# Pass 1's down projection in three parts, y evicted by halves, and a new order of the queues

## The chip, the cores and the metric

The kernel runs on one core of one Trainium2 chip. The metric is device time in microseconds, the median of three runs.

## The reference, cut to what matters

x has 4 batches of 1024 tokens with 128 features, in fp32. The block is feed-forward, mixer, feed-forward, each with a residual:

```python
x = x + 0.5 * ffn(layernorm(x))
x = x + mixer(layernorm(x))
x = x + 0.5 * ffn(layernorm(x))

def ffn(h):                      # for each batch
    logits = h.mean(axis=1) @ gate_w          # 8 experts
    top_w, top_i = top_k(softmax(logits), 2)  # one pair of experts for a batch
    for e in top_i:
        hmid = gelu(h @ w1[e] + b1[e])        # 128 -> 512
        out += weight_of(e) * (hmid @ w2[e] + b2[e])   # 512 -> 128
```

The mixer normalises, runs a causal convolution of 4 taps, silu, a projection to dt, v and gate, a rotation of v, a decaying scan over time, a mix of the heads, and an output projection.

## The kernel before

There are 8 passes: pass q is the first feed-forward of batch q for q below 4, and the second one of batch q - 4 otherwise. A pass has 8 slots, for 2 experts with 4 blocks of 128 hidden features each. Slot s = 8q + t is, on TensorE, `up(s)`: 6 matmuls of 512 columns into `hid_ps` (w1 and z are each split into a high and a low part in a shorter format, and three of the products are summed). ScalarE's `gelu(s)` evicts it into `hid`. TensorE's `down(s)` adds w2's block into `y_ps`. `down` has two forms:

- by token (`TOKEN_PASSES`, passes 0 to 4): hid is the weights operand, tile by tile, in fp32: 8 matmuls, 16 instructions. y has tokens on its partitions, as x has. GpSimd's `token_bias` adds the bias by a broadcast DMA, and VectorE's `update_x` adds y.
- feature by token: y has features on its partitions. In a slot whose place in its expert is under `PARTS[q]`, ScalarE makes `hid_hi` (`s_hi`), VectorE `hid_lo` (`s_lo`), and `down` runs three terms (high by high, low weight by high, high weight by low) in two halves. w2 is split the same way, by ScalarE (`f_split_w2`) and VectorE (`f_scale_w2`). At the end of the pass ScalarE's `pass_out` (`y_out`) evicts y into `yt` with its bias (`f_bias`), `post` (`y_turn_y`) turns it back by 8 transposes into `aux_ps`, and `update_x` (`y_update`) adds it.

The mixer of batch b runs in between, from `m_stats` to `m_add`; its matmuls and the transposes of z (`f_norm`), the routing (`f_route`) and `post` share `aux_ps`, which is handed on when its last reader is done. In the first passes all 8 experts' w1 are also split ahead (`c_pre_hi`, `c_pre_lo`, `c_pre_out`) for the later passes. `c_split_rest` splits the first pass's experts.

The order on each engine is written out by hand. Each engine walks over ticks; a slot is 40 ticks. `up(s)` and `gelu(s)` stand at tick 40 s + 40, `down(s)` at 40 s + 98, or 40 s + 132 in three parts. Everything else stands at the tick that `AT[engine][step][index]` gives. A tick isn't a time: it only orders the instructions of one engine, and semaphores do the waiting. Engines run their queues in order, so an instruction that waits holds back all behind it.

The last three slots (`TAIL`) run by token into four quarters of two tiles each, added and stored by `update_tail` and `store_quarter`.

## Time and profile before

| | us |
|---|---|
| median of 3 runs | 259.94 (259.83 to 260.12) |
| the profiled execution | 259.85 |
| its span, first to last instruction | 258.1 |
| TensorE busy | 250.5 |
| VectorE busy | 211.5 |
| ScalarE busy | 195.1 |
| GpSimd busy | 83.0 |

The profile is of one execution. An engine's busy time counts its instructions, not its waits. The granted clock of TensorE is 0.998 of full speed over the span, so 2.4 GHz nearly throughout.

### The profile page before, as it was taken

What the parts mean: (1) busy time and instruction counts of PE and PEld (TensorE: products, weight loads), DVE (VectorE), ACT (ScalarE), POOL (GpSimd) and SP (SyncE); (2) the same over time, 40 slices, a digit from 0 to 9 for tenths busy, and PEclk for the clock granted to TensorE, in tenths of its full rate; (3) what the DMA queues carried; (4) which work ended last, traced back from release to release, by engine and by line L of the source; (5) the groups of instructions that cost most, each with busy time, mean ns of one, the idle gap of its engine ahead of it and who ended that gap; (6) DMA issues with size and microseconds to landing.
All of it is one profiled execution on the core that took longest, in us unless ns stands there. A gap on an engine that the chain in (4) does not pass through costs nothing.

```text
span 258.1 us, 4609 instructions
## 1 busy us (share of the span) xinstructions
PE 250.5 (97%) x1540; PEld 217.1 (84%) x1540; DVE 211.5 (82%) x536; ACT 195.1 (76%) x236; POOL 83.0 (32%) x90
## 2 busy tenths in 40 slices
PE   7899999999999999999999999999999999999994
PEld 6879999998998979899979899888678687887893
DVE  4767587798589799999999999999999997675612
ACT  1354665866999877969848989999989957979550
...
GB/s 188 190 280 317 114 128 333 186 192 242 27 0 1 22 113 214 57 28 22 247 0 0 85 0 0 247 0 0 0 11 238 0 0 3 169 228 10 3 81 83
DMA packets 21975, 26.18 MB, mean 101 GB/s; under 512 B 1280, under 2 KB 17152, under 8 KB 21952
## 3 DMA queue, kind: packets, MB, share of 16 engines
...
q10 hardware_dynamic: 1232, 0.55, 0.8%
q8 instruction: 12, 0.20, 0.3%
...
## 4 chain that ended last, share of the span: by engine, by line
PE 90%; ACT 3%; DMA 2%; issue 2%; DVE 1%; SPq 0%; ACTq 0%
PE hid_ps L839 32%; PE y_ps L867 28%; PE y_ps L892 10%; PE aux_ps L978 5%; PE aux_ps L934 4%; PE aux_ps L1010 3%; PE aux_ps L999 3%; DMA xt<-x_dram 1%; PE hid_ps L911 1%; PE y_ps L911 1%; PE aux_ps L959 1%; ACT hid L633 1%; ACT late L723 1%; DMA m_tok<-wpack_dram 1%; PE y_ps L1022 1%
## 5 line engine op out<-in xcount | busy, mean ns | idle before, releaser
L839 PE MATMUL hid_ps<-z_hi,w_parts 128*128 128x512 f32 x256 | 83.9, 410 | 0.4 <-ACT w_parts L586 0.4
L867 PEld LDWEIGHTS y_ps<-w_sb,hid 128*128 128x128 f32 x640 | 77.1, 192 | 4.3 <-DMA w_sb<-wpack_dram 0.7
L867 PE MATMUL y_ps<-w_sb,hid 128*128 128x128 f32 x640 | 78.1, 275 | 0.3 <-ACT hid L633 0.3
L633 ACT ACTIVATE hid<-hid_ps,w_sb 128x1024 f32<-128x1024 f32 x56 | 61.8, 1109 | 16.7 <-PE hid_ps L839 16.4
L839 PEld LDWEIGHTS hid_ps<-z_hi,w_parts 128*128 128x128 f32 x256 | 45.2, 189 | 9.5 <-issue 1.4
L839 PE MATMUL hid_ps<-z_lo,w_parts 128*128 128x512 f32 x128 | 40.1, 394 | 0.0
L1217 DVE TENSOR_TENSOR hid_lo<-hid,hid_hi 128x1024 fp32r<-128x1024 f32 x19 | 22.9, 1220 | 7.8 <-ACT hid_hi L640 7.8
L839 PEld LDWEIGHTS hid_ps<-z_lo,w_parts 128*128 128x128 f32 x128 | 24.0, 188 | 5.6
L640 ACT ACTIVATE hid_hi<-hid 128x1024 fp32r<-128x1024 f32 x19 | 19.6, 1055 | 1.3 <-PE y_ps L892 1.2
L480 POOL TENSOR_SCALAR bias_tok<-w_sb,coef 128x128 f32<-128x128 f32 x10 | 7.2, 730 | 38.7 <-DMA w_sb<-wpack_dram 24.8
L1104 DVE TENSOR_SCALAR f_tok<-xt,f_mv,f_rstd 128x128 f32<-128x128 f32 x64 | 17.6, 353 | 2.0 <-POOL f_rstd L458 1.9
L1083 DVE BATCH_NORM_STATS2 f_stat<-xt 128x6 f32<-128x128 f32 x64 | 13.3, 283 | 5.7 <-DMA xt<-x_dram 5.6
L524 POOL TENSOR_SCALAR small<-mix_tmp 128x32 f32<-128x32 f32 x4 | 4.3, 1083 | 40.7 <-DVE cumd L1331 40.7
L1288 DVE SCALAR_TENSOR_TENSOR xc<-xs,vec_sb,xc 128x1024 f32<-128x1024 f32 x12 | 15.3, 1277 | 1.8 <-ACT xc L686 1.7
L468 POOL TENSOR_SCALAR f_ve<-f_mv 128x8 f32<-128x8 f32 x7 | 2.4, 343 | 43.3 <-DVE f_mv L1086 43.2
L458 POOL TENSOR_TENSOR f_rstd<-f_ve,neg_half 128x8 f32<-128x8 f32 (+1 forms) x9 | 14.6, 1624 | 3.3 <-DVE f_ve L1090 2.8
L633 ACT ACTIVATE hid<-hid_ps,b_first 128x1024 f32<-128x1024 f32 x8 | 8.9, 1110 | 6.4 <-PE hid_ps L839 6.3
L678 ACT ACTIVATE xt<-xt,m_shift,m_gain 128x128 f32<-128x128 f32 x32 | 12.7, 483 | 0.0
L892 PE MATMUL y_ps<-hid_hi,w_hi 128*128 128x512 f32 x38 | 12.5, 409 | 0.0
L892 PE MATMUL y_ps<-hid_lo,w_hi 128*128 128x512 f32 x38 | 11.9, 394 | 0.0
L892 PE MATMUL y_ps<-hid_hi,w_lo 128*128 128x512 f32 x38 | 11.9, 393 | 0.0
L1119 DVE TENSOR_TENSOR z_lo<-f_tok,z_hi 128x1024 fp32r<-128x1024 f32 x7 | 8.6, 1233 | 3.2 <-ACT z_hi L568 3.0
...
## 6 DMA issues: line engine op xcount, KB each, us to landing
...
w_sb<-wpack_dram SPq DMA_DIRECT2D x6, 258.5 KB, 4.2
...
```

What stands on the lines that cost most here:

```text
L458: nc.gpsimd.tensor_tensor(f_rstd[:, tiles], f_ve[:, tiles], neg_half[:, 0, tiles], ALU.pow).then_inc(done, 1)
L633: nc.scalar.activation(hid[:, slot % HBUF, :], hid_ps[:, slot % 2, :], ACT.Gelu, bias=bias).then_inc(hid_ready, 1)
L640: nc.scalar.activation(hid_hi[:, slot % 2, :], hid[:, slot % HBUF, :], ACT.Copy).then_inc(hid_hi_ready, 1)
L678: nc.scalar.activation(xt[:, b, t, :], xt[:, b, t, :], ACT.Identity, bias=m_shift[:, t:t + 1], scale=m_gain[:, t:t + 1]).then_inc(x_plus_h, 1)
L839: last = nc.tensor.matmul(hid_ps[:, slot % 2, cols], w, z[:, q % 2, cols], start=first, stop=end)
L867: last = nc.tensor.matmul(y_ps[:, cols], hid[:, slot % HBUF, cols], w_sb[:, q % 2, k, W2_AT + f * P:W2_AT + (f + 1) * P], start=t == 0 and ...
L892: last = nc.tensor.matmul(y_ps[:, cols], wt, src[:, cols], start=t == 0 and i == 0, stop=slot + 1 in (SLOTS * (q + 1), TAIL[0]) and end)
L978: last = nc.tensor.matmul(aux_ps[:, cols], wt[:, w, :], z[:, cols], start=first, stop=end)
L1083: V.bn_stats(f_stat[:, t, :], xt[:, b, t, :]).then_inc(f_stats_step, 1)
L1104: V.tensor_scalar(f_tok[:, t, :], xt[:, q % B, t, :], f_mv[:, t, 0:1], f_rstd[:, t:t + 1], ALU.subtract, ALU.mult).then_inc(f_norm_done, 1)
L1217: V.tensor_tensor(hid_lo[:, slot % 2, :], hid[:, slot % HBUF, :], hid_hi[:, slot % 2, :].bitcast(F32), ALU.subtract).then_inc(hid_lo_ready, 1)
L1288: V.scalar_tensor_tensor(xc[:, :], xs[:, k:k + N], conv_w[:, k:k + 1], xc[:, :], ALU.mult, ALU.add).then_inc(conv_step, 1)
```

## The change

Pass 1 leaves the passes by token, and all its slots run in three parts (`PARTS[1]` = 4). It gets `f_split_w2`, `s_hi`, `s_lo`, `f_bias` on VectorE, `y_out` and `y_turn_y`, and loses GpSimd's `token_bias`. In each pass with y feature by token, the last slot that `post` covers runs all terms of its first half before those of the second, `y_half_up` tells ScalarE that the first half is up, `pass_out` evicts y in two halves, and the next pass's `down` and `post` wait for each half by itself. The four loads of the first batch are dealt out in another way over the queues of SP and ScalarE. The last additions and stores cover 3, 2, 2 and 1 tiles instead of 2 each. Nearly all positions in `AT` are new; of them the diff shows those of the steps spoken of here.

```diff
@@ -42,90 +42,92 @@
-TOKEN_PASSES = (0, 1, 2, 3, 4)
-
-PARTS = {0: 0, 1: 0, 2: 0, 3: 0, 4: 0, 5: 3, 6: 4, 7: 4}
+TOKEN_PASSES = (0, 2, 3, 4)
+
+PARTS = {0: 0, 1: 4, 2: 0, 3: 0, 4: 0, 5: 3, 6: 4, 7: 4}
 AT = {
     "pe": {
-        "f_norm": {1: 189, 2: 389, 3: 809, 4: 1149, 5: 1509, 6: 1829, 7: 2166},
-        "m_dt": {0: 649, 1: 1029, 2: 1349, 3: 1726},
-        "m_v": {0: 689, 1: 1069, 2: 1409, 3: 1766},
-        "y_turn_y": {5: 2206, 6: 2426, 7: 2600},
+        "f_norm": {1: 169, 2: 329, 3: 849, 4: 1209, 5: 1449, 6: 1829, 7: 2166},
+        "f_route": {1: 189, 2: 369, 3: 929, 4: 1229, 5: 1529, 6: 1860, 7: 2186},
+        "m_norm": {0: 566, 1: 909, 2: 1169, 3: 1489},
+        "m_dt": {0: 749, 1: 1029, 2: 1349, 3: 1726},
+        "m_v": {0: 769, 1: 1069, 2: 1369, 3: 1766},
+        "m_gate": {0: 889, 1: 1289, 2: 1589, 3: 1926},
+        "m_out": {0: 1009, 1: 1329, 2: 1700, 3: 2048},
+        "y_turn_y": {1: 735, 5: 2086, 6: 2406, 7: 2600},
...
     "dve": {
-        "c_split_rest": {0: 90, 1: 115},
-        "c_pre_lo": {0: 309, 1: 317, 2: 366, 3: 377, 4: 490, 5: 496, 6: 502, 7: 556},
-        "f_bias": {5: 1837, 6: 2190, 7: 2383},
-        "m_stats": {0: 400, 1: 751, 2: 1057, 3: 1366},
-        "m_normalise": {0: 453, 1: 842, 2: 1146, 3: 1446},
-        "m_silu": {0: 611, 1: 998, 2: 1329, 3: 1658},
-        "m_silu_lo": {0: 640, 1: 1018, 2: 1345, 3: 1698},
-        "y_update": {0: 384, 1: 722, 2: 1028, 3: 1352, 4: 1668, 5: 2315, 6: 2515, 7: 2584},
...
+        "c_proj": {0: 112},
+        "c_split_rest": {0: 118, 1: 123},
+        "c_mixer": {0: 133},
+        "c_pre_lo": {0: 265, 1: 273, 2: 281, 3: 391, 4: 433, 5: 462, 6: 526, 7: 556},
+        "f_stats": {1: 85, 2: 219, 3: 342, 4: 1095, 5: 1355, 6: 1748, 7: 2090},
+        "f_scale_w2": {0: 147, 1: 364, 2: 754, 3: 1032, 4: 1382, 5: 1736, 6: 2046, 7: 2324},
+        "f_normalise": {1: 152, 2: 288, 3: 727, 4: 1198, 5: 1405, 6: 1823, 7: 2150},
+        "f_route": {1: 202, 2: 535, 3: 943, 4: 1262, 5: 1555, 6: 1884, 7: 2202},
+        "f_split_z": {1: 206, 2: 540, 3: 955, 4: 1307, 5: 1541, 6: 1923, 7: 2260},
+        "f_coef": {1: 259, 2: 690, 3: 978, 4: 1352, 5: 1667, 6: 1990, 7: 2315},
+        "f_bias": {1: 608, 5: 1966, 6: 2145, 7: 2462},
+        "m_stats": {0: 470, 1: 756, 2: 1044, 3: 1385},
+        "m_normalise": {0: 563, 1: 842, 2: 1152, 3: 1475},
+        "m_clip": {0: 613, 1: 947, 2: 1229, 3: 1520},
+        "m_conv1": {0: 656, 1: 968, 2: 1266, 3: 1559},
+        "m_conv2": {0: 675, 1: 982, 2: 1299, 3: 1580},
+        "m_conv3": {0: 710, 1: 992, 2: 1314, 3: 1615},
+        "m_silu": {0: 737, 1: 1009, 2: 1329, 3: 1658},
+        "m_silu_lo": {0: 749, 1: 1025, 2: 1345, 3: 1697},
+        "m_decay": {0: 781, 1: 1063, 2: 1444, 3: 1779},
+        "s_lo": {8: 445, 9: 497, 10: 511, 11: 582, 12: 593, 13: 622, 14: 696, 15: 722, 40: 1711, 41: 1768,
...
+        "y_update": {0: 399, 1: 742, 2: 1035, 3: 1371, 4: 1671, 5: 2127, 6: 2444, 7: 2584},
...
     "act": {
-        "c_split_rest": {0: 19, 1: 60},
-        "f_turn": {1: 220, 2: 426, 3: 820, 4: 1140, 5: 1506, 6: 1826, 7: 2150},
-        "m_residual": {0: 700, 1: 946, 2: 1426, 3: 1624},
-        "s_hi": {40: 1693, 41: 1706, 42: 1740, 44: 1813, 45: 1893, 46: 1906, 48: 1976, 49: 2020, 50: 2100,
...
-        "y_out": {5: 1992, 6: 2310, 7: 2540},
...
+        "c_split_rest": {0: 90, 1: 100},
+        "c_proj_hi": {0: 110},
+        "f_turn": {1: 140, 2: 330, 3: 826, 4: 1213, 5: 1420, 6: 1826, 7: 2150},
+        "f_tanh": {1: 168, 2: 496, 3: 936, 4: 1260, 5: 1546, 6: 1940, 7: 2266},
+        "f_split_w2": {1: 340, 5: 1670, 6: 1980, 7: 2300},
+        "m_scale": {0: 580, 1: 900, 2: 1146, 3: 1493},
+        "m_tap": {0: 620, 1: 928, 2: 1226, 3: 1506},
+        "m_residual": {0: 660, 1: 944, 2: 1250, 3: 1580},
+        "m_silu": {0: 666, 1: 952, 2: 1300, 3: 1613},
+        "m_silu_hi": {0: 700, 1: 980, 2: 1333, 3: 1650},
+        "m_dt": {0: 740, 1: 1020, 2: 1346, 3: 1730},
+        "m_swap": {0: 780, 1: 1060, 2: 1380, 3: 1750},
+        "s_hi": {8: 380, 9: 453, 10: 466, 11: 512, 12: 570, 13: 590, 14: 646, 15: 653, 40: 1660, 41: 1700,
...
+        "y_out": {1: 673, 5: 2030, 6: 2310, 7: 2540},
...
     "pool": {
-        "f_bias": {0: 144, 1: 375, 2: 877, 3: 974, 4: 1363},
-        "m_rms": {0: 429, 1: 791, 2: 1091, 3: 1403},
+        "f_bias": {0: 142, 2: 884, 3: 980, 4: 1354},
+        "m_rms": {0: 499, 1: 772, 2: 1064, 3: 1407},
...
     "sp": {
-        "c_pre_out": {0: 342, 1: 349, 2: 374, 3: 385, 4: 497, 5: 503, 6: 509, 7: 565},
-        "f_load": {1: 310, 2: 601, 3: 966, 4: 1207, 5: 1572, 6: 1896, 7: 2206},
+        "c_pre_out": {0: 275, 1: 282, 2: 290, 3: 402, 4: 447, 5: 472, 6: 537, 7: 564},
+        "f_load": {1: 207, 2: 569, 3: 948, 4: 1267, 5: 1560, 6: 1891, 7: 2209},
...
@@ -149,7 +151,7 @@
-    QUARTERS = 4
+    PIECES = ((0, 3), (3, 5), (5, 7), (7, 8))
...
@@ -359,11 +362,17 @@
             t = y_ps[:, :] if i < 2 else hid_ps[:, TAIL[1] % 2, :]
             return t[:, (i % 2) * HALF:(i % 2 + 1) * HALF]
 
-        def tail_ps(i):
-            return tail_bank(i // 2)[:, (i % 2) * P:(i % 2 + 1) * P]
-
-        def store_quarter(engine, i):
-            tiles = slice(i * NT // QUARTERS, (i + 1) * NT // QUARTERS)
+        def piece_of(t):
+
+            return next(i for i, (a, b) in enumerate(PIECES) if a <= t < b)
+
+        def tail_ps(t):
+
+            at = t - PIECES[piece_of(t)][0]
+            return tail_bank(piece_of(t))[:, at * P:(at + 1) * P]
+
+        def store_piece(engine, i):
+            tiles = slice(*PIECES[i])
             engine.wait_ge(x_final, i + 1)
             engine.dma_start(out[B - 1].rearrange("(t p) d -> p t d", p=P)[:, tiles, :],
                              xt[:, B - 1, tiles, :]).then_inc(out_done, 16)
@@ -414,7 +423,7 @@
                 sp.dma_start(w1_split[e], mix_tmp[:, e % PRE_BUF, :]).then_inc(pre_out[e % PRE_BUF], 16)
 
             x0 = x[0].rearrange("(t p) d -> p t d", p=P)
-            for i in range(2):
+            for i in (0, 2):
                 sp.dma_start(xt[:, 0, 2 * i:2 * i + 2, :], x0[:, 2 * i:2 * i + 2, :]).then_inc(x0_in[i], 16)
             sp.dma_start(gate_sb[:, :], gate_w).then_inc(small_in, 16)
             sp.dma_start(w1_all[:, :, 0:HEADS * P], wpack[:, :, 0:HEADS * P].rearrange("e p n -> p e n")).then_inc(w1_heads_in, 16)
@@ -659,8 +668,12 @@
                 act.wait_ge(bias2_ready, turned_passes(q + 1))
                 if turned_passes(q):
                     act.wait_ge(y_turned, 2 * turned_passes(q))
-                for i, cols in enumerate(parts_of(q, N)):
-                    act.wait_ge(hid_used, (SLOTS * (q + 1) if q < PASSES - 1 else TAIL[0]) + i)
+                for half in range(2):
+                    cols = slice(half * HALF, (half + 1) * HALF)
+                    if half:
+                        act.wait_ge(hid_used, last_turned(q) + 1)
+                    else:
+                        act.wait_ge(y_half_up, turned_passes(q + 1))
                     nc.scalar.activation(yt[:, cols], y_ps[:, cols], ACT.Identity,
                                          bias=bias2[:, q % 2, :], scale=coef[:, q % 2, 0:1]).then_inc(yt_ready, 1)
 
@@ -746,7 +759,7 @@
                 nc.scalar.activation(gated[:, :], aux_ps[:, :], ACT.Tanh, scale=0.5).then_inc(gate_tanh, 1)
 
             x0 = x[0].rearrange("(t p) d -> p t d", p=P)
-            for i in range(2, 4):
+            for i in (1, 3):
                 act.dma_start(xt[:, 0, 2 * i:2 * i + 2, :], x0[:, 2 * i:2 * i + 2, :]).then_inc(x0_in[i], 16)
             act.dma_start(vec_sb[:, :], vecs).then_inc(vecs_in, 16)
             nc.scalar.preload_act_table_set("gelu_and_others")
@@ -856,13 +869,13 @@
                         pe.wait_ge(w2_in[q % 2][k] if q else w2_head_in, 16 * (q // 2 + 1))
                 if slot == HEADS:
                     pe.wait_ge(w2_in[0][0], 16)
-                if t == 0 and q and not in_tokens(q - 1):
-                    pe.wait_ge(yt_ready, turned_passes(q))
                 if in_tokens(q):
                     pe.wait_ge(hid_ready, slot + 1)
                     for i in range(NT):
                         if t == 0 and in_tokens(q - 1) and i % (NT // 2) == 0:
                             pe.wait_ge(x_updated, 2 * q - 1 + i // (NT // 2))
+                        elif t == 0 and q and i % (NT // 2) == 0:
+                            pe.wait_ge(yt_ready, 2 * turned_passes(q) - 1 + i // (NT // 2))
                         cols = slice(i * P, (i + 1) * P)
                         last = nc.tensor.matmul(y_ps[:, cols], hid[:, slot % HBUF, cols],
@@ -881,38 +894,41 @@
                     pe.wait_ge(hid_ready, slot + 1)
                     w2 = w_sb[:, q % 2, k, W2_AT + f * P:W2_AT + (f + 1) * P]
                     terms = [(w2, hid[:, slot % HBUF, :], None)]
-                for i, (wt, src, ready) in enumerate(terms):
-                    if ready:
+                steps = [(i, half) for i in range(len(terms)) for half in range(2)]
+                if slot == last_turned(q):
+                    steps = [(i, half) for half in range(2) for i in range(len(terms))]
+                for i, half in steps:
+                    wt, src, ready = terms[i]
+                    if ready and half == 0:
                         pe.wait_ge(ready, split_slots(slot))
-                    for half in range(2):
-                        cols = slice(half * HALF, (half + 1) * HALF)
-                        end = i == len(terms) - 1
-                        if t == 0 and i == 0 and q and in_tokens(q - 1):
-                            pe.wait_ge(x_updated, 2 * q - 1 + half)
-                        last = nc.tensor.matmul(y_ps[:, cols], wt, src[:, cols], start=t == 0 and i == 0,
-                                                stop=slot + 1 in (SLOTS * (q + 1), TAIL[0]) and end)
-                        if slot == TAIL[0] - 1 and end and half == 0:
-                            last.then_inc(hid_used, 1)
+                    cols = slice(half * HALF, (half + 1) * HALF)
+                    end = i == len(terms) - 1
+                    if t == 0 and i == 0 and q and in_tokens(q - 1):
+                        pe.wait_ge(x_updated, 2 * q - 1 + half)
+                    elif t == 0 and i == 0 and q:
+                        pe.wait_ge(yt_ready, 2 * turned_passes(q) - 1 + half)
+                    last = nc.tensor.matmul(y_ps[:, cols], wt, src[:, cols], start=t == 0 and i == 0,
+                                            stop=slot == last_turned(q) and end)
+                    if slot == last_turned(q) and end and half == 0:
...
@@ -949,11 +965,9 @@
 
             def post(q):
                 free = take_aux(x_updated, 2 * q + 1, 2 * q + 2)
-                pe.wait_ge(yt_ready, turned_passes(q + 1))
                 for half in range(2):
                     free(half)
-                    if q == PASSES - 1:
-                        pe.wait_ge(yt_ready, turned_passes(q + 1) + half)
+                    pe.wait_ge(yt_ready, 2 * turned_passes(q) + 1 + half)
                     for t in range(half * NT // 2, (half + 1) * NT // 2):
                         cols = slice(t * P, (t + 1) * P)
                         last = nc.tensor.transpose(aux_ps[:, cols], yt[:, cols], ident[:, :])
@@ -1248,11 +1262,11 @@
             def update_tail():
                 q = PASSES - 1
                 xb = xt[:, q % B, :, :].rearrange("p t d -> p (t d)")
-                for i in range(QUARTERS):
-                    cols = slice(i * N // QUARTERS, (i + 1) * N // QUARTERS)
+                for i, (a, b) in enumerate(PIECES):
+                    cols = slice(a * P, b * P)
                     dve.wait_ge(tail_up, i + 1)
-                    dve.wait_ge(x_updated, 2 * q + 1 + 2 * i // QUARTERS)
-                    V.scalar_tensor_tensor(xb[:, cols], tail_bank(i)[:, 0:N // QUARTERS], coef[:, q % 2, 0:1], xb[:, cols],
+                    dve.wait_ge(x_updated, 2 * q + (1 if b <= NT // 2 else 2))
+                    V.scalar_tensor_tensor(xb[:, cols], tail_bank(i)[:, 0:(b - a) * P], coef[:, q % 2, 0:1], xb[:, cols],
                                            ALU.mult, ALU.add).then_inc(x_final, 1)
 
             def mixer_stats(b):
```

## Rows read from the trace of the kernel before

**Rows 1.** The page: busy us and share; tenths busy in 40 slices.

```profile
PE 250.5 (97%) x1540; PEld 217.1 (84%) x1540; DVE 211.5 (82%) x536; ACT 195.1 (76%) x236; POOL 83.0 (32%) x90
...
DVE  4767587798589799999999999999999997675612
```

**Rows 2.** TensorE's waits: waiting line, releaser, us in total, times, longest.

```profile
PE hid_ps L1017 <- POOL xs L449: 1.7, 1, 1.7
PE y_ps L1022 <- DVE f_tok L1104: 0.7, 1, 0.7
PE y_ps L892 <- ACT hid L633: 0.6, 1, 0.6
PE hid_ps L839 <- ACT w_parts L586: 0.4, 1, 0.4
PE y_ps L867 <- ACT hid L633: 0.3, 1, 0.3
```

**Rows 3.** By stretch: length, busy PE, PEld, DVE, ACT, POOL, clock, DMA, GB/s.

```profile
35.00:90.00 55.00, 55.00 (x380) 50.09 (x380) 44.77 (x120) 43.34 (x54) 23.33 (x27) 1.00 0.43 132
...
90.00:200.00 110.00, 109.44 (x666) 93.91 (x665) 108.07 (x242) 94.99 (x113) 45.47 (x37) 1.00 0.30 74
```

**Rows 4.** The chain in order of time: start, us, what.

```profile
61.60 1.39 PE hid_ps L839 x6
...
64.37 1.78 PE y_ps L867 x16
...
236.02 1.39 PE y_ps L892 x6
...
237.41 0.87 PE aux_ps L959 x8
```

**Rows 5.** Groups of instructions by line: count, busy us, mean ns, idle before.

```profile
L1217 DVE TENSOR_TENSOR hid_lo<-hid,hid_hi 128x1024 fp32r<-128x1024 f32 x19 | 22.9, 1220 | 7.8 <-ACT hid_hi L640 7.8
...
L640 ACT ACTIVATE hid_hi<-hid 128x1024 fp32r<-128x1024 f32 x19 | 19.6, 1055 | 1.3 <-PE y_ps L892 1.2
...
L1288 DVE SCALAR_TENSOR_TENSOR xc<-xs,vec_sb,xc 128x1024 f32<-128x1024 f32 x12 | 15.3, 1277 | 1.8 <-ACT xc L686 1.7
...
L678 ACT ACTIVATE xt<-xt,m_shift,m_gain 128x128 f32<-128x128 f32 x32 | 12.7, 483 | 0.0
...
L664 ACT ACTIVATE yt<-y_ps,bias,coef 128x1024 f32<-128x1024 f32 (+1 forms) x4 | 3.9, 990 | 0.6 <-PE y_ps L892 0.4
...
L1242 DVE SCALAR_TENSOR_TENSOR xt<-y_ps,coef,xt 128x512 f32<-128x512 f32 x10 | 7.1, 743 | 1.6 <-PE y_ps L867 1.4
```

**Rows 6.** The timeline of the first 16 us: start, us, engine, line.

```profile
3.50 0.49 DVE L1083 BATCH_NORM_STATS2 f_stat<-xt 128x6 f32<-128x128 f32 x2 [3.50 <-DMA xt<-x_dram]
...
4.23 0.49 DVE L1083 BATCH_NORM_STATS2 f_stat<-xt 128x6 f32<-128x128 f32 x2 [0.25 <-DMA xt<-x_dram]
...
13.73 0.42 ACT L603 ACTIVATE w_parts<-m_tok 128x256 fp32r<-128x256 f32 x1 [0.97 <-DMA m_tok<-wpack_dram]
...
14.06 1.10 ACT L633 ACTIVATE hid<-hid_ps,b_first 128x1024 f32<-128x1024 f32 x1
...
15.30 2.02 PE L867 MATMUL y_ps<-w_sb,hid 128*128 128x128 f32 x16 [0.33 <-ACT hid L633]
```

**Rows 7.** VectorE's timeline, 11 to 82 us.

```profile
19.15 2.56 DVE L1104 TENSOR_SCALAR f_tok<-xt,f_mv,f_rstd 128x128 f32<-128x128 f32 x8 [1.57 <-POOL f_rstd L458]
...
30.68 2.14 DVE L1104 TENSOR_SCALAR f_tok<-xt,f_mv,f_rstd 128x128 f32<-128x128 f32 x8
...
41.53 1.65 DVE L1261 BATCH_NORM_STATS2 m_stat<-xt 128x6 f32<-128x128 f32 x8
```

**Rows 8.** The timeline of the last 6 us.

```profile
253.82 0.93 DVE L1255 SCALAR_TENSOR_TENSOR xt<-hid_ps,coef,xt 128x256 f32<-128x256 f32 x2
```

**Rows 9.** DMA from 246 us: GB/s in 40 slices; issue, KB, us to landing.

```profile
GB/s 288 289 291 291 213 0 0 0 0 0 0 0 0 0 0 0 0 0 0 0 0 0 0 0 0 0 0 108 266 264 295 279 291 251 2 5 0 0 0 0
...
out_dram<-xt ACTq DMA_DIRECT2D x2, 128.0 KB, 2.4
```

98 lines of the change are left out of this document (39 added, 59 removed), and 3 rows, old and new, of the table AT.

## The prediction

> **What bounds the kernel now.** I began with the page [rows 1]. TensorE is busy 250.5 us, 97% of the span. The reader should see in the same group that VectorE's row of tenths is at 9 in nearly every slice from the fifteenth to the thirty-first. The list of TensorE's waits [rows 2] then accounts for what is idle: 1.7 us before the first instruction, 0.7, 0.4 and 0.3 us in the first 15 us, and 0.6 us once more, late. What remains lies behind the last matmul. So TensorE sets the time, and either its work must shrink or one of these few waits must go. Third, the busy times by stretch [rows 3]: from 90 to 200 us VectorE is busy 108.07 of 110 us, from 35 to 90 us 44.77 of 55. TensorE is the bound with a second engine right behind it. Whoever gives VectorE work can spend 10.2 us before 90 us and almost nothing for 110 us after that.
>
> **TensorE's work.** The chain is made of TensorE pieces, so prices are read off it [rows 4]. An up projection of a slot is 1.39 us, a down projection by token (16 instructions) 1.78 us. In three parts it is 6 instructions and 1.39 us. Eight slots of pass 1 change from the one to the other: 8 x (1.39 - 1.78) = -3.12 us. Pass 1's y now lies feature by token, so `post(1)` turns it back: 8 transposes, 0.87 us [rows 4]. Sum **-2.25 us**.
>
> **Work that TensorE does not see at once.** VectorE gets eight `hid_lo` (1220 ns each [rows 5], start to start about 1.14 us): 9.1 us, two `w2_lo` instead of one scaling, some 0.8 us, and `f_bias` 0.3 us, together 10.2 us. That is as large as its whole idle time from 35 to 90 us [rows 3]. ScalarE gets eight `hid_hi` (1055 ns [rows 5]), two `w2_hi` of 0.6 us, and two halves of `yt` (990 ns is the mean over both forms [rows 5]; I take 0.6 us a half), together 10.8 us, against 11.7 us idle between 35 and 90. GpSimd loses one `token_bias` and its broadcast DMA, which nobody waited for. All this is free only where each operand comes in time, so I followed the queues through the new positions, with the durations of before. A wait counts from the end of one instruction to the start of the next.
>
> **The start.** Before, tiles 0-1 and 2-3 of x follow each other on SP's queue; VectorE starts the first at 3.50 and the third tile at 4.23, idle 0.25 us for its DMA [rows 6]. Now the two loads go out on SP and ScalarE at the same moment, as tiles 0-1 and 4-5 did. Gain 0.25 us (bounds 0 and 0.35). Then: ScalarE's `gelu(0)` ran at 14.06, behind the copy at 13.73 that waited 0.97 us for the expert's weights, and TensorE started at 15.30 after 0.33 us of waiting for it [rows 6]. `c_split_rest` now stands behind `gelu(0)` and `gelu(1)`, so gelu(0) can run from some 13.35 us on. The first down projection's own weights were landing at about the same time, so I take 0.15 of the 0.33. Sum **-0.4 us**, bounds -0.1 and -0.65.
>
> **The waits that the walk finds.** From there, on an axis of the new kernel:
> 1. `f_turn` of pass 1 stands before `gelu(3)` on ScalarE; `down(3)` waits 0.15 us.
> 2. Up to slot 9: `lo(8)`, `c_pre_lo` 5, the first mixer's statistics (eight instructions, 1.65 us, [rows 7], and eight short ones) and `lo(9)` come in this order on VectorE and end at 47.7; `down(9)` is at its third term at the same moment: 0.1 us.
> 3. VectorE then has lo(10), a pre-split, the route, `split_z`, a pre-split and the eight instructions of `m_normalise`(0), of the kind that takes 2.14 us for eight [rows 7], and ends at 53.65. TensorE is at `m_norm` at 52.4, needs the last tile, and loses 0.55 us; lo(11) right behind it costs 0.1 us more.
> 4. `lo(14)` stands behind conv1, conv2 (about 1.25 us each [rows 5]) and the coefficients: 63.5, where `down(14)` reaches its third term at 63.2. 0.4 us.
> 5. The border of passes 1 and 2. ScalarE has, in this order, hi(15), eight residual instructions (3.1 us, [rows 5]), tanh, the two halves of `yt`, gelu(16). TensorE has down(15), post(1), down(16). The second half of yt can't start before down(15) has ended (66.9 on the walk). Then 0.6 us of yt, 1.1 us of gelu [rows 6], and the hand-overs: down(16) starts at 69.1, while post(1) fills 0.87 us. **1.3 us** idle. This one is in the order of the queues and not in a race: it would be some 1.1 us with a ScalarE that is on time. Behind the waiting yt stand gelu(16), silu_hi and gelu(17).
> 6. The projection for dt reaches its third term at 71.4, silu_lo ends at 71.5, with VectorE late from y_update(1): 0.25 us.
> 7. ScalarE's two table loads, the swap and `f_turn`(3) put gelu(20) at 87.5; down(20) loses 0.4 us.
>
> Sum 0.15 + 0.1 + 0.65 + 0.4 + 1.3 + 0.25 + 0.4 = **+3.25 us**. At down(23) VectorE is 0.7 us later than before at the same work. Each of these but the fifth is a difference of two chains some 50 us long, so each could be 0 or twice as much. Bounds for the sum: 1.1 (the fifth alone) and 5.2.
>
> **From 100 us on.** The order of VectorE's and ScalarE's instructions is changed here too, with almost no room [rows 3]. Work is the same but for one scaling done earlier. Gain possible: the wait of 0.6 us [rows 2]. Loss possible: the 0.7 us of lateness met again in full, and about as much from the new order, 1.5 us. I take 0. The halves of yt in passes 5 and 6 cost ScalarE 0.2 us each, where it has room; the wait that they could take from TensorE is not there, since rows 2 have none.
>
> **The end.** The last four additions were 256 columns each and just kept step with the quarters: the last two start at 253.82 and take 0.93 us together [rows 8]. Now they have 384, 256, 256 and 128 columns. From 0.48 us for 256 and 743 ns for 512 [rows 5, 8] I get 0.61, 0.48, 0.48, 0.35. The first can start 0.22 us later than before and each follows the last: they end 0.24 us later than before. The last store is half as large. At 250 to 295 GB/s, the rates of the stores' stretch [rows 9], 64 KB less is 0.22 to 0.26 us. The sum is 0 (bounds -0.2 and +0.3). The issue's 2.4 us to landing for 128 KB [rows 9] halved would save 1.2 us; I don't take that, since most of the 2.4 us isn't transfer at that rate.
> The Trainium skill's page "DMA: Bandwidth & Descriptors" (section "Anatomy of one DMA — SWDGE (gpsimd) path") puts about 2.0 us of a DMA down to setup and completion whatever its size. By that a last store of 64 KB saves only its transfer, and the sum stays; without it, at the full 1.2 us, the sum would be 1 us lower. The trace agrees so far: 2.4 us is far more than 128 KB need at the rates shown.
>
> **The sum** on the profiled span: 258.1 - 2.25 - 0.4 + 3.25 + 0 + 0 = 258.7, so +0.6. I take off 0.15 for waits that the walk may count twice, since a wait moves all engines' work closer together: +0.45. The profiled execution took 259.85 us, the median is 259.94: the forecast is **260.4 us**, a tie or a shade slower.
>
> **Rivals.**
> - *The cover holds* (0.32). The walk's differences of 0.1 to 0.65 us vanish, and only the border of passes 1 and 2 costs its 1.1 to 1.3. For it: VectorE and ScalarE have just enough idle time between 35 and 90 us [rows 3], and start-to-start times are under the durations that the list gives. Against it: it needs all of that idle time. 258.1 - 2.25 - 0.4 + 1.2 gives -1.45: **258.5 us**.
> - *VectorE becomes the bound* (0.18), on the other side. It enters the stretch 90 to 200 us late by 0.7 us or more, and each instruction that TensorE needs there comes late by that. It decides as soon as the lateness exceeds the lead that VectorE had, which no row shows; TensorE never waited for it. +0.45 + 1.5: **261.9 us**. What speaks for it is 1.9 us of idle time in 110 us. GpSimd may add to it: eight normalising instructions took 2.56 us beside GpSimd's work and 2.14 us without [rows 7]. The Trainium skill's page "SBUF — State Buffer" (section "Who interferes with whom") says that a VectorE instruction with two SBUF inputs and a GpSimd instruction that reads SBUF exclude each other for their whole length; `hid_lo` is of that kind, and by that rule the new work slows GpSimd and is slowed by it. The two lengths in the trace are no proof of it, and nothing in the sum uses it.
> - *The cheaper slot is really 0.39 us less and half of the waits go, the late 0.6 us too* (0.08): **259.3 us**.
> - The change not doing what it says is excluded: late passes run this same form at 1.39 us [rows 4].
>
> **Chances and range.** The forecast holds 0.42, with its own range 259.7 to 261.2. The noise bound is 0.2%, 0.52 us, about what a measurement of this kernel can tell: 259.4 to 260.5 is no change. Of the forecast 0.22 lies within it and 0.20 above; the first rival is faster (0.32), the second slower (0.18), the third split in two. Faster 0.36, same 0.26, slower 0.38. The range is from 258.0, the first rival with the full gain at the start, to 262.2, the second with a bound more.
>
> **What would show it.** Pass 1's down pieces of 6 instructions and 1.39 us. TensorE's busy time near 248.2 us. In its list of waits, lines for `yt` and gelu(16) at about 67 to 69 us with over 1 us together, and some tenths each for hid_lo, f_tok or m_tok, and silu_lo between 45 and 88. VectorE's idle time from 35 to 90 us near 3 us, not 10. The first store no later, the last addition 0.2 to 0.3 us later after the last matmul. I am wrong if TensorE has under 1 us idle between 35 and 100 us, or if new waits of over 1 us stand behind 100 us.

## The result

The changed kernel takes 261.88 us (four runs: 261.38, 261.42, 262.33, 262.35) against 259.88 (259.79 to 260.12) before: ratio 1.0071, interval 1.0059 to 1.0082, so 1.8 us slower. The forecast was 260.4 us, the range 258.0 to 262.2. The profiled execution took 261.42 us, its span is 259.4, 1.3 more than before. Ratios here and below are of means, so two medians need not give them exactly.

The page of the changed kernel, as [rows 1]:

```profile
PE 251.6 (97%) x1468; PEld 212.2 (82%) x1468; DVE 221.2 (85%) x547; ACT 205.7 (79%) x250; POOL 84.4 (33%) x86
...
DVE  4796959998989999999999999999999999666612
```

72 matmul instructions went, and yet PE is busy 1.1 us longer: ends of matmuls are modelled, and a matmul that stands before a short wait is drawn out over part of it. The busy sum can't show the saving. Its list of waits, as [rows 2]:

```profile
PE y_ps L910 <- ACT hid L642: 0.6, 1, 0.6
PE aux_ps L973 <- ACT yt L677: 0.5, 1, 0.5
PE y_ps L910 <- DVE hid_lo L1231: 0.4, 2, 0.3
PE y_ps L880 <- ACT hid L642: 0.4, 1, 0.4
PE y_ps L880 <- issue: 0.4, 1, 0.4
```

The first of these was there before; the other four are new (hid_lo at 47.9 and 63.8 us, yt at 67.8, the issue at 69.4, gelu's hid at 87.9). By stretch, as [rows 3]:

```profile
35.00:90.00 55.00, 53.27 (x300) 43.88 (x299) 48.89 (x116) 51.56 (x62) 26.09 (x22) 1.00 0.21 80
90.00:200.00 110.00, 109.35 (x666) 93.03 (x665) 107.40 (x238) 94.89 (x112) 42.54 (x39) 1.00 0.31 73
```

By this count TensorE was never idle from 35 to 90 us before; now it is for 1.73 us. ScalarE has 3.4 us of room left there instead of 11.7, VectorE 6.1 instead of 10.2. The chain at the border of passes 1 and 2, as [rows 4]:

```profile
52.78 1.40 PE aux_ps L950 x8
...
62.93 3.08 ACT xt L691 x8
66.01 0.63 ACT silu L706
...
66.86 0.77 ACT yt L677
...
67.77 1.23 PE aux_ps L973 x8
69.00 0.39 issue
69.39 2.02 PE y_ps L880 x16
```

The 8 transposes of mixer 0 (L950) take 1.40 us where 0.87 is their work: they wait tile by tile for VectorE. From 60 to 67.6 us the chain runs over ScalarE.

To find every wait, the smeared ones too, I kept a ledger: the moment at which each up projection starts, less the work of all TensorE pieces before it, at the prices of [rows 4] (1.39 for an up projection or a slot in parts, 1.78 by token, 0.87 for transposes). What is left is waiting, give or take some 0.08 us at a single slot, since a piece's step to the next depends a little on what follows. The table gives the changed kernel's minus that of the kernel before, in us, at each slot where it moves.

```
up(0)  -0.48     up(14) +0.73     up(33) +3.54
up(2)  -0.75     up(17) +1.19     up(41) +4.16
up(5)  -0.47     up(18) +2.70     up(51) +4.56
up(11) -0.41     up(22) +3.07     tail   +4.25
up(12) +0.04     up(24) +3.52
```

So: the start gives 0.75 us, the work 2.30, and the waits from up(2) on cost 5.00, of which 4.27 arise before up(24) at 99 us. The last matmuls (those of the tail) start 1.95 us later. Behind them the kernel gains 0.60: the span is longer by 1.34 (258.05 and 259.39), and 0.60 + 1.34 = 1.94. The timeline of the changed kernel's end, as [rows 8]:

```profile
255.09 1.01 DVE L1269 SCALAR_TENSOR_TENSOR xt<-y_ps,coef,xt 128x384 f32<-128x384 f32 x2 [3.39 <-PE y_ps L927]
...
256.02 0.74 DVE L1269 SCALAR_TENSOR_TENSOR xt<-hid_ps,coef,xt 128x256 f32<-128x256 f32 x2
```

Its last addition ends at 256.76, 2.64 us before the span does. Before, it ended at 254.75 [rows 8], 3.30 us before it.

### The profile page after: what moved, and what is told of

It reads as the page before. It is cut to its first block, busy times and chain, and to the rows that moved or that the text cites. A ratio compares the mean times of both kernels' runs of the same rounds, so it can differ in the third digit from the quotient of the medians.

```text
span 259.4 us, 4503 instructions
## 1 busy us (share of the span) xinstructions
PE 251.6 (97%) x1468; PEld 212.2 (82%) x1468; DVE 221.2 (85%) x547; ACT 205.7 (79%) x250; POOL 84.4 (33%) x86
## 4 chain that ended last, share of the span: by engine, by line
PE 67%; ACT 12%; DVE 9%; issue 7%; POOL 3%; ACTq 0%; DVEq 0%; POOLq 0%
PE hid_ps L852 24%; PE y_ps L880 14%; PE y_ps L910 12%; PE aux_ps L1024 3%; PE aux_ps L1013 3%; PE aux_ps L992 3%; ACT hid L642 3%; PE aux_ps L950 3%; ACT xt L691 2%; POOL small L533 2%; PE hid_ps L1031 2%; PE aux_ps L973 1%; ACT late L736 1%; DVE m_stat L1275 1%; PE y_ps L927 1%
## 5 line engine op out<-in xcount | busy, mean ns | idle before, releaser
L880 PEld LDWEIGHTS y_ps<-w_sb,hid 128*128 128x128 f32 x512 | 60.8, 192 | 4.4 <-issue 2.3
L880 PE MATMUL y_ps<-w_sb,hid 128*128 128x128 f32 x512 | 63.0, 276 | 0.9 <-ACT hid L642 0.4
L1231 DVE TENSOR_TENSOR hid_lo<-hid,hid_hi 128x1024 fp32r<-128x1024 f32 x27 | 32.7, 1217 | 5.5 <-ACT hid_hi L649 5.5
L649 ACT ACTIVATE hid_hi<-hid 128x1024 fp32r<-128x1024 f32 x27 | 28.0, 1055 | 2.6 <-PE y_ps L910 2.4
L489 POOL TENSOR_SCALAR bias_tok<-w_sb,coef 128x128 f32<-128x128 f32 x8 | 9.2, 1161 | 31.6 <-DVE coef L1200 20.9
L910 PE MATMUL y_ps<-hid_lo,w_hi 128*128 128x512 f32 x54 | 17.7, 400 | 0.4 <-DVE hid_lo L1231 0.4
L910 PE MATMUL y_ps<-hid_hi,w_hi 128*128 128x512 f32 x54 | 17.8, 402 | 0.0
L910 PE MATMUL y_ps<-hid_hi,w_lo 128*128 128x512 f32 x54 | 17.4, 394 | 0.0
L910 PEld LDWEIGHTS y_ps<-hid_lo,w_hi 128*128 128x128 f32 x54 | 9.8, 188 | 4.1 <-DVE hid_lo L1231 2.1
L573 ACT ACTIVATE f_tok<-aux_ps 128x1024 f32<-128x1024 f32 x7 | 7.2, 1024 | 6.8 <-PE aux_ps L950 6.8
```

The costliest lines, as they stand in the source:

```text
L489: nc.gpsimd.tensor_scalar(bias_tok[:, k, :], w_sb[:, q % 2, k, B2_ROWS:B2_ROWS + D], coef[:, q % 2, k:k + 1], None, ALU.mult).then_inc(bia ...
L649: nc.scalar.activation(hid_hi[:, slot % 2, :], hid[:, slot % HBUF, :], ACT.Copy).then_inc(hid_hi_ready, 1)
L880: last = nc.tensor.matmul(y_ps[:, cols], hid[:, slot % HBUF, cols], w_sb[:, q % 2, k, W2_AT + f * P:W2_AT + (f + 1) * P], start=t == 0 and ...
L910: last = nc.tensor.matmul(y_ps[:, cols], wt, src[:, cols], start=t == 0 and i == 0, stop=slot == last_turned(q) and end)
L1231: V.tensor_tensor(hid_lo[:, slot % 2, :], hid[:, slot % HBUF, :], hid_hi[:, slot % 2, :].bitcast(F32), ALU.subtract).then_inc(hid_lo_ready, 1)
```

## The experiments

Times are compared by ratio, since the kernel before took 259.71 to 260.14 us on the chips used.

**1. The changed kernel again (`after_again`).** No edit.

> The changed kernel as it stands, as the base for the runs beside it. Two of its four times were 261.4 us and two 262.3 us, with spans of 259.4 and 260.4 us. If that is a second level of this kernel, it shows again among these runs, and the profile says where the 1.0 us lies. If it came from the chip, all runs here agree with each other. Expected ratio to before 1.006 to 1.010.

Measured: 262.31 us (261.48 to 262.90), ratio 1.0085 (1.0069 to 1.0102). It stays slower, and spreads over 1.4 us. The two executions differ at the very start. TensorE's timeline of this one, and then of the one above:

```profile
1.73 5.83 PE L1031 MATMUL hid_ps<-ones 128*128 128x128 f32 x26 [1.73 <-POOL xs L458]
7.39 0.33 PE L1036 MATMUL y_ps<-ones,f_tok 128*128 128x64 f32 x2
```

```profile
1.73 4.86 PE L1031 MATMUL hid_ps<-ones 128*128 128x128 f32 x26 [1.73 <-POOL xs L458]
6.53 0.41 PE L1036 MATMUL y_ps<-ones,f_tok 128*128 128x64 f32 x2
```

The same 26 instructions end 0.9 us later. Taken one by one, they follow each other at 0.21 us up to some moment and at 0.11 us from then on: in the run above the moment was 5.3 us, and in this one it had not come when the last of the 26 began, at 7.2. Up to there TensorE had done nothing but these. VectorE's first normalised tile was ready at 6.4 and 6.5 us, so the late case makes everything wait (up(0) at 12.25 instead of 11.45). At up(5) the two ledgers differ by 0.4 us more (f_norm(1) is met late), and from there to the tail by 0.25. A time of this kernel can be compared to better than 1 us only where the start is known, which is why the rest is read from the ledger. The times by themselves can't rank kernels 1, 2, 4 and 12, whose ratios' intervals overlap.

**2. Pass 1 by token in the new order (`token_in_new_order`).**

```diff
-TOKEN_PASSES = (0, 2, 3, 4)
+TOKEN_PASSES = (0, 1, 2, 3, 4)
-PARTS = {0: 0, 1: 4,
+PARTS = {0: 0, 1: 0,
```

and without the steps of the form in parts; `f_bias(1)` is on GpSimd again.

> The changed kernel with pass 1 by token again (GpSimd's bias at tick 375), all other new positions, loads and pieces kept. First theory: the loss is TensorE waiting for operands of VectorE and ScalarE around pass 1, 3.5 us net at 102 us, against 2.3 us of saved work. Then the work comes back (+2.3) and nearly all these waits go: span 257.0 to 257.8 us, which is 0.3 to 1.1 us under before, from the start (0.75) and the end (0.6). Rival: the new order of the mixer and the routing loses the time whatever pass 1 does; then the span stays at 259 us or above, with waits at the places where they are now.

Measured: 262.44 us (262.11 to 263.33), ratio 1.0101 (1.0081 to 1.0120). The theory fell. The rival holds for the time, and for the places of the waits only in part. The ledger at the tail is 9.42 us, against 6.10 before and 10.35 in the changed kernel. From up(5) to up(17) the changed kernel gathers 1.6 us, and this one none. The waits at down(9), at mixer 0's transposes and at down(14) come with the form. (Kernel 2 also waits 0.6 us at up(4), as the changed kernel did in kernel 1's execution but not in its first.) From up(17) on it gathers 3.4 us, and the border costs 1.45 us here too, in another way. TensorE's list and VectorE's timeline of this kernel:

```profile
PE y_ps L876 <- DVE xt L1252: 1.2, 1, 1.2
```

```profile
66.25 2.15 DVE L1114 TENSOR_SCALAR f_tok<-xt,f_mv,f_rstd 128x128 f32<-128x128 f32 x8
68.30 1.23 DVE L1304 SCALAR_TENSOR_TENSOR silu<-silu,xc 128x1024 f32<-128x1024 f32 x1
69.44 1.42 DVE L1252 SCALAR_TENSOR_TENSOR xt<-y_ps,coef,xt 128x512 f32<-128x512 f32 x2
```

down(16) waits for y's addition, which stands behind the norm of pass 3 and mixer 0's silu on VectorE. In the kernel before, mixer 0 was through its silu earlier (place 611 against 737) and the norm of pass 3 stood at 650 instead of 727. The new order alone costs over 3 us with pass 1 by token; in that order the form in parts gains 2.3 us of work and pays 0.9 us of waits, 1.3 if the slots up to up(5) are left out. That net gain is read from the ledger and from two profiled spans with the same start, 260.8 and 259.4. The medians show 0.1 us of it (262.44 and 262.31), and the intervals overlap.

**3. The late places of before (`late_order_old`).** In the changed kernel, all places beyond 1040 that both kernels have are set to those of before.

> The changed kernel with the old positions wherever both the old and the new one lie behind tick 1040 (about 105 us on). In the trace 0.7 us of waits net appear between 140 and 225 us. Theory of order: they come from the new late positions and go: 0.7 us less than the changed kernel. Rival, lateness: VectorE enters that stretch later than before in any order, and they stay or move: within 0.3 us of the changed kernel.

Measured: 264.99 us (263.55 to 266.02), ratio 1.0184 (1.0157 to 1.0212). Both theories fell. Counted from its own start, the ledger is the changed kernel's up to up(27) within 0.2 us, and then jumps by 3.7 and 0.6 us at up(28) and up(29), where the two orders meet: TensorE stands still for 2.7 us before the transposes at 120.25, and the granted clock is 0.50 (1.2 GHz) from 119.8 to 123.2 us. The halves of two orders don't join there. Behind the jump the ledger is flat up to up(58): with the late places of before, neither the wait at up(41) nor the one at up(51) is there. So much speaks for the theory of order (see kernel 11).

**4. No low part of hid in pass 1 (`no_low_part`).** The third term reads `hid_hi` instead of `hid_lo`, and the eight `hid_lo` are left out, so pass 1's y lacks the low part of hid.

```diff
-terms = [(hi, h_hi, hid_hi_ready), (lo, h_hi, None), (hi, h_lo, hid_lo_ready)]
+terms = [(hi, h_hi, hid_hi_ready), (lo, h_hi, None)] + (
+    [(hi, h_hi, None)] if q == 1 else [(hi, h_lo, hid_lo_ready)])
```

> The changed kernel without the eight hid_lo of pass 1: the third term of pass 1 reads hid_hi again, so the low part of hid is left out there and TensorE's work is the same. Theory that VectorE's load makes the waits before the border: the waits at about 48, 53 and 64 us (1.6 us together) go, the border of passes 1 and 2 keeps 1.0 to 1.4 us, and the time falls by 1.8 to 2.5 us, since the later waits on late VectorE work shrink too. Rival, ScalarE's load makes them: the time falls by under 0.6 us.

Measured: 261.85 us (261.61 to 262.52), ratio 1.0081 (1.0065 to 1.0098). The waits at down(9) and down(14) went, 0.99 us together, mixer 0's stayed at 0.7, and at the border TensorE now waits longer for `yt`:

```profile
PE aux_ps L970 <- ACT yt L673: 1.0, 1, 1.0
```

At up(19) the ledger is still 0.37 us under the changed kernel's, from up(25) on 0.15, from up(30) on nothing, and both tails start at 250.6 us (this one had started 0.17 us later). The theory, 1.8 to 2.5 us less, fell, and the time lies where the rival put it. Taking 9 us of work off VectorE gives next to nothing at the end: in front of the border the chain runs over ScalarE.

**5. The two ends alone (`ends_alone`), 6. the last pieces alone (`pieces_alone`), 7. the first loads alone (`loads_alone`).** All on the kernel before. 5 has these edits, 6 the pieces, 7 the loads (the first two lines are SyncE's; ScalarE's loop changes from `range(2, 4)` to `(1, 3)`; what uses PIECES is left out here):

```diff
-            for i in range(2):
+            for i in (0, 2):
-        "c_split_rest": {0: 19, 1: 60},
+        "c_split_rest": {0: 90, 1: 100},
-    QUARTERS = 4
+    PIECES = ((0, 3), (3, 5), (5, 7), (7, 8))
```

> The kernel before, pass 1 by token and its own orders kept, with only the small parts of the change: x's four first loads dealt in turn to two queues, ScalarE's first weight splits behind gelu(0), and the last additions and stores as three, two, two and one tiles. Theory (the two ends give what the ledger of the changed kernel shows, 0.75 us at the start and 0.65 at the end, and nothing later takes it back): span 256.6 to 257.1 against 258.1, time 258.5 plus or minus 0.4, faster than before by 0.4 to 0.7%. Rival (my prediction's own sizes, 0.4 at the start and nothing at the end): 259.4. Second rival (the order of the queues written out for the slower start does not use the earlier one: the gain goes into the first waits for VectorE near 13 us): 259.5 to 259.9.

> The kernel before with the last additions and stores as three, two, two and one tiles instead of four pairs, and nothing else. Theory (the last store of 64 KB lands sooner than one of 128 KB by more than the addition before it comes later): the last addition ends 0.2 to 0.3 us later after the last matmul, the span ends 2.6 to 2.7 us after it instead of 3.35, and the time falls by 0.4 to 0.6 us, to about 259.3. Rival (my prediction: the two cancel): 259.8 to 259.9, no change.

> The kernel before with x's four first loads dealt in turn to SyncE's and ScalarE's queues, and nothing else. Theory (the start's gain is mostly the loads' alone): the first up projection starts 0.3 to 0.5 us sooner than at 11.92 us, and the time falls by as much, to 259.4 to 259.6. Rival (the first norm waits for the third and fourth group whichever queue brings them, all of them ending together): 259.8 to 259.9, first up projection at 11.8 to 11.9.

Measured, in that order: 259.07 us (258.82 to 259.84), ratio **0.9966 (0.9952 to 0.9979)**; 259.82, ratio 0.9991 (0.9982 to 1.0000); 259.56, ratio 0.9980 (0.9971 to 0.9989). So 0.9, 0.2 and 0.5 us, the first a little under its theory's 0.4 to 0.7%. The start is as the theory had it: with the loads alone up(0) stands at 11.37 us against 11.92, with the change of pace among the first multiplications at 4.7 and 4.6 us. The end is between theory and rival: from the tail's first matmul to the end of the span it is 9.35 us before, 9.11 and 9.12 with the pieces, 8.75 in the changed kernel. The difference lies in the last store. DMA rows of 5 from 246 us, then the changed kernel's:

```profile
out_dram<-xt SPq DMA_DIRECT2D x1, 64.0 KB, 2.6
```

```profile
out_dram<-xt SPq DMA_DIRECT2D x1, 64.0 KB, 2.2
```

Why the same store lands 0.4 us later in the one kernel, I have not found. It isn't the form or the order: the long landing is also in kernel 4, which has both, and the short one in kernels 2, 3, 8, 9 and 12. The kernel with both ends alone beats the one before and the changed one.

**8. Mixer 0's residual later (`residual_later`).**

```diff
-        "m_residual": {0: 660,
+        "m_residual": {0: 790,
```

> The changed kernel with one position other: mixer 0's eight residual activations on ScalarE (3.1 us in a row) stand behind gelu(21) at 89 us, where ScalarE has a gap of 1.2 us, instead of before silu and the eviction of y at 62.8. Theory (ScalarE's queue at the border of passes 1 and 2 makes TensorE wait, 1.5 us there and 0.6 at gelu(20)): waits gathered up to up(18) fall from 2.7 to 1.7 to 2.1, the time falls by 0.6 to 1.2 us against the changed kernel as it is (261.4 to 262.3), to about 261.0, unless the 3.1 us put into 89 us make a wait of their own near 90, of 0.3 to 1. Rival (what ends the border's waits is VectorE's chain of convolutions or TensorE's own transposes): waits at up(18) stay within 0.3 of 2.7, and the time stays or rises by the new wait near 90 us, 262 to 263.

One correction to it: place 790 is not behind gelu(21). The residual stands behind mixer 0's swap and in front of gelu(20), at 80.9 us. For the border this makes no difference.

Measured: 264.77 us (264.47 to 265.60), ratio 1.0182 (1.0165 to 1.0199). The theory fell. The border costs 1.51 us, as in the changed kernel, with ScalarE idle for 2 us in front of it:

```profile
66.18 1.06 ACT L702 ACTIVATE silu<-xc 128x1024 f32<-128x1024 f32 x1 [1.99 <-DVE xc L1298]
67.94 1.45 ACT L673 ACTIVATE yt<-y_ps,bias,coef 128x512 f32<-128x512 f32 x2 [0.69 <-PE y_ps L906]
69.28 1.11 ACT L638 ACTIVATE hid<-hid_ps,w_sb 128x1024 f32<-128x1024 f32 x1
```

The first half of `yt` waits for TensorE itself (0.69 us for y_ps). So the residual's 3.1 us cost nothing where they stood. At their new place they are passed on in full: gelu(20) and the turn of pass 3's z come late, and the ledger rises by 3.1 us more than the changed kernel's at up(21) and up(22). ScalarE has no room there.

**9. The form in parts in the old order (`parts_in_old_order`).** The changed kernel with the places of before; only what the form adds has new places, and `f_scale_w2(1)` and `f_split_w2(1)` stand behind the old `f_coef(1)`.

> The changed kernel's code (pass 1 in three parts, both ends) with the places in the queues of the kernel before; only what the new form itself adds has the changed kernel's places (the high and low parts of hid 8 to 15, the split of the second weights behind their ratio, the eviction of y, its transposes and addition, mixer 0's second projection and the swap behind them). It is the fourth of a table of two forms and two orders: by token in the old order 259.1 us, by token in the new order 262.4, in parts in the new order 261.4 to 262.3. Theory (the new order costs 3.3 us by itself, and the form saves 2.3 us of TensorE's work for 2 to 3 us of waits at down(9), at mixer 0's transposes and at the border of passes 1 and 2): 258.6 to 260.0 us. Rival (the two are no sum: three parts without the later mixer 0 make VectorE's chain of mixer 0 collide with the low parts of hid, and every wait that the new order avoids comes back): 261.5 to 264.

Measured: 279.35 us (278.31 to 280.73), ratio 1.0750 (1.0724 to 1.0777). The rival had the direction, far too small. TensorE's waits and VectorE's timeline:

```profile
PE y_ps L906 <- DVE hid_lo L1227: 11.5, 3, 6.8
```

```profile
39.15 1.64 DVE L1252 SCALAR_TENSOR_TENSOR xt<-y_ps,coef,xt 128x512 f32<-128x512 f32 x2 [1.42 <-PE y_ps L876]
...
41.97 1.64 DVE L1271 BATCH_NORM_STATS2 m_stat<-xt 128x6 f32<-128x128 f32 x8
...
44.06 1.61 DVE L1093 BATCH_NORM_STATS2 f_stat<-xt 128x6 f32<-128x128 f32 x8
...
46.14 1.19 DVE L1227 TENSOR_TENSOR hid_lo<-hid,hid_hi 128x1024 fp32r<-128x1024 f32 x1
```

Two sets of statistics stand in front of lo(8) and down(8) loses 2.9 us, which delays all that feeds on it; and waits of 1.8, 2.6 and 6.8 us follow. Some of the loss isn't waiting: in three stretches the granted clock is 0.50 (1.2 GHz), and TensorE is busy for 13.7 us of them (last section), so that the same work at 2.4 GHz would take about 6.8 us less, by my estimate. So form and order are no sum: by token the old order is better by 3.3 us, in parts it is worse by 17. As in kernel 3, places of two orders are mixed here; an old order with places fitted to the form was not run.

**10. Fewer first multiplications (`ends_less_warm`).** On kernel 5:

```diff
-    WARM_EARLY, WARM_SUM, WARM = 13, 2, 6
+    WARM_EARLY, WARM_SUM, WARM = 9, 2, 6
```

> The kernel before with both ends of the change, and with 9 of TensorE's 13 multiplications of ones ahead of the first norm (18 instructions instead of 26). In the ten profiles so far the step from one such instruction to the next falls from 0.21 to 0.11 us at a moment that differs from run to run, 4.6 to 7.4 us into the span; where it comes late the 26 end at 7.4 us, 1.1 us after the first normalised tile is there, and the first up projection starts at 12.4 instead of 11.4 us. Theory (the count of these multiplications makes the late case dear): the 18 end at 5.8 us at the slow step; the late case starts its first up projection at 11.8 to 12.0, the spread of the times shrinks from 1.0 to some 0.5 us, the median falls to 258.6 to 258.9. Rival (with less work ahead of it TensorE's step comes later still, and the first transposes or up projections run at the slow step): first up projection at 12.4 or later, time 259.3 to 260.5.

Measured: 259.09 us, ratio 1.0000 (0.9979 to 1.0022), in two groups: seven runs from 258.79 to 259.10 and five from 260.73 to 261.02. Kernel 5's ratio is 0.9966, so on the mean this is worse. The early case is as good as with 13, and the late one costs 1.9 us instead of 0.9. That is the rival's direction, for part of the runs. The profiled run is of the first group, so where the second loses its time isn't shown.

**11. The late places of the new order alone (`late_new_order`).** Kernel 5 with the changed kernel's 79 other places beyond 1600.

> The kernel before with both ends of the change and, beyond place 1600 (from about 147 us on, passes 4 to 7 and mixer 3), the changed kernel's 79 other places; all before it as before. Theory (the 0.7 us of waits that the changed kernel gathers between 140 us and the end come with its late order, not from what is late before it): waits between up(37) and the last additions rise by 0.4 to 0.8 us against the kernel with both ends alone, time 259.5 to 259.9. Rival (they come from passes 1 and 2, handed on through a mixer or a transfer that is late): waits there the same within 0.2 us, time 258.9 to 259.2.

Measured: 259.38 us (259.06 to 260.20), ratio 0.9989 (0.9980 to 0.9998). With up(0) at 12.38 and 12.39 us in the two profiles, the ledger rises at the tail from 6.26 to 6.67, all of it at up(51): the theory's lower end. The chain of this kernel, then of kernel 5:

```profile
205.39 1.72 PE aux_ps L1003 x4
207.10 0.09 issue
207.19 2.02 PE aux_ps L1014 x16
```

```profile
205.34 1.72 PE aux_ps L1003 x4
207.06 1.39 PE y_ps L896 x6
208.45 1.78 PE aux_ps L1014 x16
```

Place 2048 instead of 2066 for `m_out(3)` puts mixer 3's output projection right behind its heads (L1003), with no down projection between them, and it waits for VectorE to gate them. The changed kernel has the same 0.4 us at up(51). Its other late wait, 0.5 us at up(41), is not in this kernel, and the traces show why. `m_residual(3)` stands at 1580 in the changed kernel, in front of gelu(39), and at 1624 here as before, behind it. ScalarE's timeline of the changed kernel, then of the one before:

```profile
165.19 3.18 ACT L691 ACTIVATE xt<-xt,m_shift,m_gain 128x128 f32<-128x128 f32 x8
168.27 1.10 ACT L642 ACTIVATE hid<-hid_ps,w_sb 128x1024 f32<-128x1024 f32 x1
```

```profile
164.90 1.11 ACT L633 ACTIVATE hid<-hid_ps,w_sb 128x1024 f32<-128x1024 f32 x1
...
166.94 3.18 ACT L678 ACTIVATE xt<-xt,m_shift,m_gain 128x128 f32<-128x128 f32 x8
```

gelu(39) ends at 169.37 us and down(39) starts at 169.42, 0.25 late. In all 14 profiles the wait at up(41) goes with the place: it is there in the six kernels that have 1580 (the changed one, 1, 2, 4, 8 and 12), and in none of the eight that have 1624. No run changes this place alone.

**12. y evicted whole (`y_whole`).** On the changed kernel, for passes 1, 5 and 6:

```diff
+                if q < PASSES - 1:
+                    act.wait_ge(hid_used, last_turned(q) + 1)
+                    nc.scalar.activation(yt[:, :], y_ps[:, :], ...).then_inc(yt_ready, 2)
+                    return
-                if slot == last_turned(q):
+                if slot == last_turned(q) and q == PASSES - 1:
```

> The changed kernel with the eviction of y undone: in passes 1, 5 and 6 the last slot's products run term by term and one activation of 128x1024 evicts y, as in the kernel before; pass 7 stays by halves, and all else stays changed. It tests the 1.5 us at the border of passes 1 and 2, where the changed kernel's gelu(16) stands behind the two halves (66.86 to 68.29 us) on ScalarE, ends at 69.3, and down(16) starts at 69.39. Theory (down(16) waits for gelu(16), not for the transposes, so that halves buy nothing there: the whole eviction starts 0.3 us later and takes 0.3 less): down(16) starts within 0.2 us of the changed kernel's, counted from the first up projection; waits at up(18) stay at 2.6 to 2.9 us over those of the kernel before; time 261.2 to 262.5, the same. Rival (the halves hide most of the eviction behind the last slot's second half at all three borders, and without them each border costs 0.5 to 0.9 us more): down(16) 0.5 to 0.9 us later, time 262.5 to 264.

Measured: 262.49 us (262.48 to 262.69), ratio 1.0096 (1.0082 to 1.0110). Counted from up(0), the border of passes 1 and 2 costs 0.29 us more than with halves, that of pass 5 nothing, that of pass 6 0.32: half of what the rival expected, more than the theory's bound. ScalarE's timeline and TensorE's:

```profile
67.80 1.20 ACT L673 ACTIVATE yt<-y_ps,bias,coef 128x1024 f32<-128x1024 f32 x1 [0.43 <-PE y_ps L915]
68.90 1.10 ACT L642 ACTIVATE hid<-hid_ps,w_sb 128x1024 f32<-128x1024 f32 x1
```

```profile
69.14 1.06 PE L978 MATMUL aux_ps<-ident,yt 128*128 128x128 f32 x8 [1.47 <-ACT yt L673]
70.11 2.02 PE L885 MATMUL y_ps<-w_sb,hid 128*128 128x128 f32 x16
```

down(16) starts 0.11 us after gelu(16) ends (70.00), as in the changed kernel (69.29 and 69.39). By the ledger the halves help by 0.6 us. The ratios' intervals of this kernel and the changed one overlap. Half of it is gained at the border of passes 6 and 7, where the kernel before waited 0.27 us at up(59) and the changed one doesn't.

## Why the prediction was nearly right

- **TensorE's work, -2.25 us: right.** The pieces are there at 1.39 us and post(1) at 0.87; the ledger's sum is 2.30. The sign by which I meant to see it, PE busy near 248.2 us, was wrong: it shows 251.6. So was the one for VectorE's idle time from 35 to 90 us, near 3 us: it is 6.1. VectorE's busy time rose by 9.7 us over the span, near the 10.2 that I took, but 4.8 of it lie in front of 35 us, where the new order puts more of its other work.
- **The start, -0.4 us: mis-sized.** It gave 0.75, beyond my bound of 0.65: 0.48 at up(0), from the loads (kernel 7), and 0.27 from gelu(0) before the copies, where I had credited 0.15 of it. What I did not see is that TensorE's first multiplications can take the gain back, by up to 0.9 us, and do so in some runs.
- **The waits up to 100 us, +3.25 us: mis-sized.** They are 4.27, inside the bounds. One by one, forecast and ledger: down(3) 0.15 and 0.28, of which 0.1 comes back behind it; down(9) 0.1 and 0.45; mixer 0's transposes with lo(11) 0.65 and 0.69; lo(14) 0.4 and 0.46; the border 1.3 and 1.51; the projection for dt 0.25 and 0.07; gelu(20) 0.4 and 0.56, and behind it 0.45 more at up(23) and up(24). Taken off is a wait of 0.25 us of the kernel before at up(21) that went. The 0.15 that I took off for double counting was not there. The largest misses are the 0.45 at up(23) and up(24), which the walk didn't have, and VectorE's late statistics at slot 9.
- **The border as an order and not a race: right.** Kernel 8 freed ScalarE in front of it and kernel 4 freed VectorE, and it did not shrink (1.51 and 1.94 us). The order down(15), yt, gelu(16), down(16) with 0.87 us of transposes to fill it is what costs, and kernel 12 shows down(16) tied to the end of gelu(16) either way.
- **From 100 us on, 0: wrong by 0.7.** 0.41 us is `m_out(3)`'s place (kernel 11). 0.49 at up(41) goes with `m_residual(3)`'s place in front of gelu(39) (also kernel 11), though no run moved it alone. Against both stand 0.28 gained at up(59) by the halves of y, a gain that I had put at nothing because TensorE's list showed no such wait: it was there, spread over longer matmuls. The last 0.1 us is at up(34) and open. The 0.7 us of lateness that I carried for VectorE's queue did not come back as waits: the ledger is flat from up(24) to up(33), so the rival "VectorE becomes the bound" came near the time (261.9) by a mechanism that isn't there.
- **The end, 0: wrong by 0.60 in the changed kernel.** The additions end only 0.07 us later after the tail's first matmul instead of 0.24, and the time behind them falls by 0.66. Kernel 6 gives 0.23 of it. The 2.4 us to landing that I read was the median of two stores, 1.9 and 2.9; the last one, the one that counts, took 2.9 before and 2.2 in the changed kernel, 2.6 in kernel 6. The fixed 2.0 us quoted from the Trainium skill (page "DMA: Bandwidth & Descriptors") stand in its section on the GpSimd path, while these stores go out on SyncE's and ScalarE's queues. The trace agrees with it in this: most of a landing, 2.2 us or more, doesn't shrink with the bytes.
- **What I argued too weakly:** the new order counted only as the road on which the form's waits arise. Kernel 2 against kernel 5 shows what it costs by itself with pass 1 by token: 3.3 us. I had priced the walk without asking what the same order would do to the old form. How much of the changed kernel's own waits is the order's can be said only in part. The 1.6 us up to up(17) come with the form, since kernel 2 has none. The 1.5 us of the border have a reason of their own in each of the two kernels. The 1.55 us behind it are there with either form (2.0 in kernel 2).
- **The third rival's time: added up wrongly.** Its terms (half of the waits, and the 0.6 us gone) give 258.1 - 2.25 - 0.4 + 1.6 - 0.6, or 258.3 us by median, and not 259.3. By 258.3 its whole chance of 0.08 would have been one for faster.

Summed: -0.75 - 2.30 + 4.27 + 0.73 - 0.60 = +1.35 us of span, against the +0.45 forecast. That it came this near is in part luck: the waits up to 100 us cost 1.2 us more than I took, and the two ends gave 0.95 more. The time, 1.8 us over that of before, is beyond the forecast's own range (up to 261.2) and within the whole one. The median lies 0.5 us above the profiled run; two of the four executions took 1 us more than the other two, as a late start would make it (kernel 1), but they have no trace.
